# A two-layer model on one core: the shared experts' sums come back into another buffer, and the searched order of the instructions is replaced

## The reference, cut to what matters

```
sh_mid = gelu(einsum('th,ehd->ted', xt, Wsh_up))
shared_out = einsum('ted,edh->th', sh_mid, Wsh_down)
...
routed_out = einsum('ted,edh->th', rt_mid * gate[:, :, None], Wrt_down)
return shared_out + routed_out
```

## Time and profile before

| | us |
|---|---|
| runs: median (lowest to highest) | 1294.34 (1285.93 to 1298.04) |
| the profiled execution's own time | 1290.69 |
| its span, first to last instruction | 1288.9 |
| TensorE busy in the span | 1176.2 (91%) |
| VectorE / GpSimd / ScalarE busy | 1062.3 (82%) / 869.4 (67%) / 841.6 (65%) |
| mean granted TensorE clock | 0.972 of full speed |

### The profile page before, as it was taken

The page is one execution under the profiler, slowest core; times in us unless marked ns, Lnnn a source line. Parts: engine busy times, 40 slices in busy tenths (PEclk is TensorE's granted clock), DMA queues, the critical chain, the costliest instruction groups (busy, mean ns, idle before and its releaser), DMA issues.

```text
span 1288.9 us, 28774 instructions
## 1 busy us (share of the span) xinstructions
PE 1176.2 (91%) x9866; PEld 987.2 (77%) x9866; DVE 1062.3 (82%) x2365; ACT 841.6 (65%) x2393; POOL 869.4 (67%) x1101
## 2 busy tenths in 40 slices
PE   8899889788986999998999899989999999899996
PEld 7665446666875888887888888878788889788885
DVE  5797236968799899888989799888799898789778
ACT  4013643657765678776778767868777878587775
POOL 3123442657778887787887788875888797776636
PEclk9899979989998999999999999999999999999998
DMA  7942102224334637345646364545355563645342
GB/s 232 244 140 67 55 27 95 66 54 106 90 97 106 184 66 217 106 150 141 171 104 193 93 195 112 177 142 166 75 175 147 151 157 109 176 120 155 93 130 69
DMA packets 219493, 165.95 MB, mean 129 GB/s; under 512 B 103572, under 2 KB 186772, under 8 KB 219348
## 3 DMA queue, kind: packets, MB, share of 16 engines
q1 hardware_dynamic: 214612, 149.82, 41.9%
q0 software_dynamic: 4736, 14.29, 3.9%
HBM read 115.71 MB, written 48.16 MB: 127 GB/s over the span
## 4 chain that ended last, share of the span: by engine, by line
PE 39%; DVE 19%; POOL 10%; DMA 10%; issue 8%; ACT 7%; SPq 5%; DVEq 0%; POOLq 0%; another core or an unknown queue 0%; ACTq 0%
PE ps L1359 12%; DMA XYLM<-parked 4%; SPq L1305 4%; DVE yv L2168 3%; DMA WK<-in_WK 3%; PE ps L1757 3%; DVE KQ L2168 2%; PE ps L1421 2%; PE ps L1632 2%; PE ps L1694 1%; PE ps L1724 1%; PE ps L1710 1%; PE ps L1765 1%; PE ps L1467 1%; DVE Mp L2047 1%
## 5 line engine op out<-in xcount | busy, mean ns | idle before, releaser
L2576 ACT ACTIVATE XYLM<-ps 128x512 f16<-128x512 f32 x216 | 125.3, 600 | 54.7 <-PE ps L1667 54.0
L2168 DVE SCALAR_TENSOR_TENSOR yv<-ps,cw,yv 128x511 f32<-128x511 f32 (+2 forms) x192 | 142.8, 745 | 6.5 <-ACT yv L2512 2.7
L2168 DVE SCALAR_TENSOR_TENSOR KQ<-ps,cw,KQ 128x511 f32<-128x511 f32 (+2 forms) x192 | 140.6, 743 | 8.4 <-ACT KQ L2512 6.0
L1359 PE MATMUL ps<-XH,WVh 128*128 128x256 f32 (+1 forms) x384 | 134.6, 351 | 3.3 <-DVE O L2367 1.8
L1359 PE MATMUL ps<-XH,WVl 128*128 128x256 f32 (+1 forms) x384 | 123.6, 322 | 0.0
L1359 PE MATMUL ps<-XL,WVh 128*128 128x256 f32 (+1 forms) x384 | 123.5, 322 | 0.0
L2610 ACT ACTIVATE sq<-O 128x128 bf16<-128x128 f32 x256 | 79.4, 310 | 58.3 <-DVE O L2348 20.1
L2616 ACT ACTIVATE O<-O,small 128x128 f32<-128x128 f32 x256 | 82.6, 408 | 22.4 <-POOL small L2854 21.9
L2298 DVE TENSOR_TENSOR ZL<-ps,cst 128x256 f16<-128x256 f32 x192 | 77.7, 417 | 21.0 <-PE ps L1653 19.5
L2873 POOL TENSOR_TENSOR OGL<-O,OGH 128x512 fp32r<-128x512 f32 x62 | 81.1, 1308 | 5.2
L1359 PEld LDWEIGHTS ps<-XH,WVh 128*128 128x128 f32 x384 | 73.6, 192 | 8.2 <-DVE O L2367 1.9
(11 more groups left out here) (359 smaller groups left out, 4072.6 us busy)
## 6 DMA issues: line engine op xcount, KB each, us to landing
XYLM<-parked SPq DMA_DIRECT2D x56, 512.0 KB
RC<-crow SPq DMA_DIRECT2D x128, 128.0 KB
decayed<-PTE SPq DMA_DIRECT2D x64, 256.0 KB
PT<-decayed SPq DMA_DIRECT2D x64, 256.0 KB
parked<-LM SPq DMA_DIRECT2D x56, 256.0 KB
WV<-in_WV SPq DMA_DIRECT2D x16, 512.0 KB, 4.1
exr<-in_ex SPq DMA_DIRECT2D x16, 384.0 KB, 4.3
WK<-in_WK SPq DMA_DIRECT2D x16, 256.0 KB, 4.7
```

What stands on the lines that cost most here:

```text
L1359: m = pe.matmul(o, a, b, start=c + k == 0, stop=c == 1 and k == 2)
L2168: m = dve.scalar_tensor_tensor(out=dst[:, k:512], in0=ps[:, bk, 0:512 - k], scalar=cw[:, h, j, 3 - k:4 - k], in1=dst[:, k:512], op0=ALU.mu ...
L2576: leave(act.activation(changed(u, k), ps[:, bank("b", u, k), :].rearrange("p (c n t) -> p c n t", c=2, t=1 << (k - 1)), ACT.Copy), "b", u, k)
```

## The change

1. `fld` no longer loads into the memory of `WVh` but into the key and query memory of head 13, `KQ[:, 1]`. It waits for the last product that reads this memory, `KS` of unit 55 (head 13's last chunk), in both batches; before, it waited for all `cv` and `Zt` projections of heads 14 and 15. Its rank in the plan is the same. `WVh` stays where it is.
2. In the plan, the costs of three parts of the block inverse are raised: `iv1` from 3.6 to 3.9, `p8` from 1.15 to 1.55, `q8` from 1.15 to 1.6 us. The instructions are the same.
3. `GRAIN` goes from 0.09700 to 0.0517, and all of `RANK` and `LATER` is replaced. The new numbers are from a search over replays in which the DMAs' landing times are spread at random. So every list, of every engine, can have another order, and the PSUM banks follow. No instruction is added or removed by this.

```
-    GRAIN = 0.09700
+    GRAIN = 0.0517
...
-    P.add(("iv1", h), rank + 0.1, ("DVE", 3.6, (("dg", h), "DMA"), (("xc", h - 1), "ACT") if h > LEAD else None,
+    P.add(("iv1", h), rank + 0.1, ("DVE", 3.9, (("dg", h), "DMA"), (("xc", h - 1), "ACT") if h > LEAD else None,
...
-    P.add(("p8", h), rank + 0.1, ("POOL", 1.15, (("iv1", h), "DVE")))
+    P.add(("p8", h), rank + 0.1, ("POOL", 1.55, (("iv1", h), "DVE")))
...
-    P.add(("q8", h), rank + 0.1, ("POOL", 1.15, (("iv2", h), "DVE")))
+    P.add(("q8", h), rank + 0.1, ("POOL", 1.6, (("iv2", h), "DVE")))
...
-    weights = [(("cv", h, v, b), "PE") for h in (HK - 2, HK - 1) for v in range(2) for b in range(2)]
-    weights += [(("Zt", h, n), "PE") for h in (HK - 2, HK - 1) for n in (0, 2, 4, 6)]
-    P.add(("fld",), 4 * HK - 8, ("SP", 6.0, *weights))
+    P.add(("fld",), 4 * HK - 8, ("SP", 6.0, *[(("KS", 4 * HK - 9, b), "PE") for b in range(2)]))
...
-        total, WVh = twins("total", "WVh", [128, 2, 2, 512])
-        total = total[:].rearrange("p a c n -> p (a c n)").rearrange("p (n d) -> p n d", n=NT)
+        WVh = sb("WVh", [128, 2, 2, 512], F32R)
...
+        total = KQ[:, (HK - 3) % 3].rearrange("p k t -> p (k t)").rearrange("p (n d) -> p n d", n=NT)
...
-                    for k in (HK - 2, HK - 1):
-                        for b in range(2):
-                            w.wait_ge(*full("cv", k, 0, b))
-                            w.wait_ge(*full("cv", k, 1, b))
-                        for n in range(0, NT, 2):
-                            w.wait_ge(*full("Zt", k, n))
+                    for b in range(2):
+                        w.wait_ge(*full("KS", 4 * HK - 9, b))
```

Three entries of the tables, as they were and as they become, show the kind of change:

```
-    "ck3": {"DVE": 1725.51}
+    "ck3": {"DVE": 253.77}
-    "ld": {"DMA": -0.42, "SP": -1480.26}
+    "ld": {"DMA": -180.19, "SP": -410.02}
-    "fup": {"SP": 1.33}
+    "fup": {"POOL": 169.77, "SP": -539.82}
```

More of the change, by code:

```diff
@@ L104 @@
[L104 to L113, removed]
@@ L119 @@
[L119 to L128, removed]
[3 rows of a table removed]
@@ new lines @@
+    "iv1": {"DVE": -424.93}, "iv2": {"DVE": -224.76}, "iv3": {"DVE": -443.76}, "kb": {"POOL": 171.24},
+    "kb:first": {"POOL": 14.23}, "kn": {"ACT": 1374.77, "POOL": 134.84},
+    "kn:first": {"ACT": 275.87, "PE": -156.91, "POOL": -308.37}, "kns": {"ACT": -780.5},
+    "kns:first": {"ACT": -329.63}, "ld": {"DMA": -180.19, "SP": -410.02}, "ld:last": {"DMA": 45.92, "SP": 283.5},
+    "ln1": {"ACT": -20.84, "DVE": 222.58, "PE": -88.46}, "ls": {"DMA": 81.69, "SP": -20.91},
+    "ls:last": {"DMA": 56.89, "SP": 366.03}, "max": {"SP": 2.19}, "mk:0": {"POOL": 433.31}, "mk:1": {"POOL": 219.74},
@@ new lines @@
+    "ov:1": {"DVE": -366.86, "PE": 232.57}, "own": {"DVE": -429.99}, "p1:0": {"DVE": -68.36, "PE": -121.26},
+    "p1:1": {"DVE": 27.26}, "p8": {"POOL": -213.19}, "pd": {"DMA": 325.19, "SP": -895.26},
+    "pd:first": {"DMA": 175.96, "SP": 517}, "pd:last": {"DMA": 313.5, "SP": -493.56},
+    "pf": {"DVE": 172.9, "SP": 243.4}, "pl": {"POOL": 6.37}, "pl:first": {"POOL": 15.59}, "pl:last": {"POOL": -36.33},
+    "pm": {"POOL": 68.09}, "pm:first": {"POOL": 634.35}, "pm:last": {"POOL": 639.07},
+    "pre": {"ACT": -830.11, "DVE": 94.48}, "ps": {"DMA": -177.84, "SP": 3.21},
@@ new lines @@
+    "ps:first": {"DMA": -267.15, "SP": -317.62}, "ps:last": {"DMA": 20.34, "SP": 735.5}, "pt:last": {"DVE": -311.51},
+    "pv:0": {"PE": 8.46}, "pv:1": {"PE": -666.95}, "py": {"POOL": 1261.98}, "py:first": {"POOL": 206.17},
+    "q8": {"POOL": 6.96}, "r": {"DVE": -581.63}, "r:first": {"DVE": -65.75, "PE": -1765.17},
+    "r:last": {"DVE": -57.39, "PE": -1050.4}, "rb:0": {"SP": -298.18}, "rc:0": {"DVE": 1012.4},
+    "rc:1": {"DVE": -121.62}, "rd:0": {"SP": 78.63}, "rd:1": {"SP": 210.21}, "row": {"DMA": -531.58},
@@ new lines @@
+    "row:first": {"DMA": -85.8, "SP": -250.3}, "row:last": {"DMA": 241.31, "SP": -1186.17}, "rt1": {"DVE": 298.72},
+    "sT": {"ACT": -139.9, "PE": 3.29}, "sc:0": {"ACT": -400.63, "PE": 0.38}, "sc:1": {"ACT": 450.62, "PE": -125.1},
+    "sd": {"DVE": 1296.02}, "slot": {"DVE": -98.48, "PE": -539.68}, "so": {"DVE": -153.94, "PE": -273.42},
+    "so:first": {"DVE": 578.75, "PE": -1724.17}, "so:last": {"DVE": 0.93, "PE": -188.84}, "spg": {"POOL": -19.8},
+    "sq": {"ACT": 298.13, "POOL": -483.87}, "sq:first": {"ACT": 126.75}, "sq:last": {"ACT": 593.63},
@@ new lines @@
+    "U:first": {"ACT": 0.06}, "U:last": {"PE": 0.25}, "Vt": {"ACT": 0.38}, "Vt:first": {"ACT": 0.21},
+    "am:0": {"POOL": 0.76}, "am:1": {"POOL": 0.36}, "b:last": {"ACT": 0.25}, "c:last": {"PE": 0.14},
+    "cb": {"DMA": 1.91, "DVE": 0.84}, "ck1:first": {"DVE": 0.07}, "ck3": {"DVE": 0.03}, "ck:first": {"ACT": 0.7},
+    "cnt": {"PE": 0.1}, "cq": {"ACT": 0.04}, "cq:first": {"PE": 0.01}, "crow": {"ACT": 1}, "cv": {"ACT": 0.02},
+    "cv2": {"DVE": 0.27}, "cv2:first": {"DVE": 0.12}, "dd:0": {"SP": 0.2}, "dec": {"POOL": 0.03},
@@ new lines @@
+    "dec:first": {"POOL": 0.12}, "dec:last": {"ACT": 0.04}, "dg": {"DMA": 0.06, "SP": 0.2}, "dn": {"DVE": 0.08},
+    "exg:0": {"ACT": 0.89, "DVE": 0.37}, "exg:1": {"ACT": 0.63, "DVE": 0.71}, "exv:1": {"PE": 0.02},
+    "fWK": {"POOL": 0.23, "SP": 0.15}, "fWO": {"POOL": 0.25}, "fin": {"DVE": 0.26, "SP": 5.15}, "fld": {"SP": 1.61},
+    "fs": {"ACT": 0.58}, "fup": {"SP": 1.55}, "fx": {"POOL": 0.83, "SP": 1.85}, "gg": {"DVE": 0.25},
+    "gram:last": {"DVE": 0.09}, "gt": {"ACT": 0.15}, "kb": {"POOL": 0.3}, "kb:first": {"POOL": 0.9},
@@ new lines @@
+    "kn": {"POOL": 0.12}, "kn:first": {"PE": 0.01, "POOL": 1.14}, "kns": {"ACT": 0.02}, "kns:first": {"ACT": 0.1},
+    "ld": {"DMA": 0.08}, "ld:last": {"DMA": 0.13, "SP": 0.09}, "ln1": {"ACT": 0.04, "DVE": 0.1},
+    "ls:last": {"SP": 1.86}, "nr2": {"DVE": 0.06}, "oc:0": {"ACT": 0.43}, "ol:last": {"POOL": 0.37},
+    "on": {"ACT": 0.2}, "op": {"DVE": 0.05}, "os": {"POOL": 0.02}, "os:last": {"POOL": 0.58},
+    "ot:first": {"PE": 0.01}, "ot:last": {"DVE": 0.47, "PE": 0.4}, "pd": {"DMA": 0.11}, "pd:first": {"SP": 2.09},
@@ new lines @@
+    "pd:last": {"DMA": 0.66, "SP": 2.67}, "pf": {"DVE": 0.64}, "pl:first": {"POOL": 0.05}, "pl:last": {"POOL": 0.75},
+    "ps": {"DMA": 0.34}, "ps:first": {"DMA": 1.8, "SP": 0.14}, "ps:last": {"SP": 1.51}, "py:first": {"POOL": 0.06},
+    "rb:0": {"SP": 2.21}, "rb:1": {"SP": 0.6}, "rc:0": {"DVE": 0.53}, "rd:0": {"SP": 0.58}, "rd:1": {"SP": 2.44},
+    "row": {"SP": 0.47}, "row:first": {"SP": 3.25}, "row:last": {"DMA": 0.31, "SP": 1.09}, "sc:0": {"ACT": 0.44},
+    "sd": {"PE": 0.01}, "slot": {"PE": 0.33}, "small": {"SP": 0.46}, "so:first": {"DVE": 0.02},
@@ L185 @@
+    "so:last": {"DVE": 0.27, "PE": 0.3}, "spg": {"POOL": 1.06}, "sq:first": {"ACT": 0.13},
+    "sq:last": {"ACT": 0.34, "POOL": 0.19}, "sr": {"DMA": 0.44, "POOL": 0.17}, "sw": {"DMA": 0.12},
+    "sx": {"SP": 0.53}, "tp": {"DVE": 1.69}, "up": {"ACT": 0.36}, "x1": {"DVE": 0.1}, "xb": {"SP": 3.52},
+    "xi:first": {"POOL": 0.14}, "y:last": {"DVE": 0.73, "PE": 0.35}, "yl:last": {"DVE": 0.37, "PE": 0.22},
 }
```

95 lines of the change are left out of this document (31 added, 64 removed), and 27 rows, old and new, of tables (LATER, RANK).

## The result

| | before | after |
|---|---|---|
| runs, median (lowest to highest), us | 1293.59 (1285.93 to 1298.04) | 1229.97 (1228.63 to 1230.73) |
| the profiled execution / its span | 1290.69 / 1288.9 | 1230.72 / 1228.9 |
| mean granted TensorE clock | 0.972 | 0.982 |

The account below looks back on a forecast made before the run. TensorE's throughput was taken to bound the middle, the state chain of head 15 and VectorE's and GpSimd's lists the end. 1290.7 - 6 - 4 = 1280.7, on the median's scale 1284; range 1267 to 1306.

Parts of the forecast that it names:

- Part 3: All lists: the new numbers move everything and remove nothing; taken as 0 us, between -43 and +14.
- part 2: Block inverse: raised costs stop TensorE's `a` being placed too early; -4 us, between 0 and -10.4.
- The end of -43: Middle: all 14 windows like the best one, TensorE idle 13.6 us in place of 56.2.
- The waits that were read: TensorE's waits in the middle: landing of inverse matrices 12.7 us in 9, scaled output 12.5 us in 9.
- Part 1: Tail: the load of the shared sums moves up to 69 us earlier; -6 us, between 0 and -10.6.
- the stop of 10.85 us: GpSimd's wait in front of its ninth gather in the tail, which the early load was to remove.
- the seven us between them: Tail: `U` of unit 63 was to follow unit 62's after 5.87 us, not 12.83, so 7.0 us sooner.
- the inverse does not take the gain away as long as VectorE and ScalarE serve it at once: Unit 63's inverse: levels of 1.7 us each, 7.4 us in all, ready at 1262.6 at the earliest.
- the rival of the larger gain: Landing waits to a quarter, scaled-output waits halved, tail gives 10.6 us: 1268 us; chance 0.22 of below 1278.
- Slower: Rival: TensorE's `a` waits for its matrices in every head, 1312 us; chance 0.16 of above 1300.
- The sum fails outright if the busy middle itself gets longer or shorter by more than 10 us: Written test on the middle: a change of more than 10 us either way refutes the forecast sum.
- Extra table loads: ScalarE: silus ahead of the last gates or decays need up to three more loads, 3.8 us, halving the gain at worst.

Follow-up runs that it names:

- a_oldfld: After with the old load of the shared sums, also in the plan, so all lists were made anew with the new numbers: 1243.06 us, ratio 0.9630 to before.
- b_weights: Before without the 28 key/query and output weight loads from head 2 on and without the waits for them; GpSimd's work stays: 1264.73 us, ratio 0.9842.
- b_all: Before without weight loads from head 2 on, with half of each `XYLM` load and `p8`, `q8` on 384 of 512 elements: 1256.98 us, ratio 0.9772.
- b_early: Before's lists, TensorE's untouched, with `fld` in head 13's key memory and gathers, additions, silus and preliminary sums moved forward: 1294.63 us, ratio 1.0039.
- a_late: After's lists, TensorE's untouched, with the old load's memory and wait; gathers, additions, silus and preliminary sums moved behind it: 1245.87 us, ratio 0.9645 to before.
- b_thin: Before's lists with GpSimd's `p8` and `q8` on 384 of 512 elements, so each takes about 1.15 us: 1288.74 us, ratio 0.9975.

## Why the prediction was wrong

- **Part 3, the new numbers: the step that failed.** It took 0, within -43 to +14. Measured: 48 us of 61 with the old load (`a_oldfld`), which holds the new costs of part 2 as well. Choosing the mean of the old windows, "the nearest row", was no argument: the row says what the old order does. The end of -43 was nearly right for the middle, which gave 45.0 us with 86 matmuls fewer in it. The rest was looked for nowhere: the 15 us ahead of head 2, where GpSimd's weight waits were 14.4 us in 3 (1.2 in after) and `b_weights` wins 10.2. Nor did it count that the plan itself could be shorter (20 us), or that busy time shrinks (735.8 to 731.6 to 729.1 for the same matmuls from before to `b_weights` to `b_all`).
- **The waits that were read.** The prediction took the waits of the bounding engine and weighed `XYLM`, 12.7 us. The landings that cost most were those where GpSimd stood, 40.8 and 9.7 us, one view further. Their price shows in the growth of the lag; TensorE's waits for `O` carried only a part of it (12.5 to 6.3 us in the middle of `b_weights`).
- **Part 1: the load came early, what it was to free did not follow.** It was issued at 1126, behind a `KS` of unit 55 that is earlier like all else, additions started at 1136, and of the stop of 10.85 us one of 4.6 is left. But VectorE is busy 33.5 of the last 39 us, where under 30 was expected, `U` of 63 comes 9.2 us after `U` of 62 and not 6, and in `b_early` the seven us between them did not go. Before's own plan has 13.8 us there, so the order itself held the gap. The sentence that failed is "the inverse does not take the gain away as long as VectorE and ScalarE serve it at once": they serve in list order, as TensorE does, and a level took 4.0 to 4.6 us, not 1.7; 4.7 and 5.0 stood in the trace of before. The tail is 0.1 us longer in after. What the early load buys is that head 15's projections may stand in the tail, 11 us by `a_late`, 13 to 15 of the whole by the ratios of `a_oldfld` and `a_late`, an effect the rival of the larger gain named without a price.
- **Part 2: the reason for the -4 fell, the size is open.** `b_thin` gives 0.9975 with an interval that holds 1 and the 4 us, and the waits for `XYLM` stay. It makes the steps as short as planned; the new costs by themselves were not run.
- **The rivals.** That of the larger gain was nearest, with the right sentences (landing waits to a quarter, scaled output halved; both fell further, to 0.2 and 3.4) and an end of 1268, since it counted no more than these waits and the tail's idle time. Slower: its condition, `XYLM` waits above 19 us, turned out 0.2. The test written down, "The sum fails outright if the busy middle itself gets longer or shorter by more than 10 us", is what happened, by 45.
- **Extra table loads** at the silus did not come: one, as before. Their price by the row, 3.8 of 6 us, would have been more than the half that was written.

## What to carry to other kernels

Where an engine works through a list in order, look at the distance between a load and the step that waits for it, on every engine and not only on the one that bounds. A planner that takes one fixed landing time can put the waiting step exactly there (13 of 14 heads with the old numbers, 4 with the new), although its result is wanted long after, and each late landing can then pass to what follows; put such a step some microseconds behind the landing, or let the search see spread landing times. Where a change replaces a whole order, compare the execution with the order's own plan, head by head: the difference that grows points at what the plan did not foresee. And do not take the busiest engine's idle time for all of it: of the 28 us between before's middle and `b_all`'s, with the same work, 6.7 came out of what was counted as TensorE's busy time.

## What the runs showed of the hardware

The same load of 256 KB took from 2.7 to 6.7 us from issue to landing in one execution, and 2.6 to 6.3 in the other; the DMA engines' share in the middle was 0.52 and 0.54. In after's tail the mean granted clock was 0.96 with TensorE busy 35.9 of 42.8 us, in before's 0.86 with 32.2 of 42.8, in `a_late`'s 0.87 with 40.8 of 54.2, in `a_oldfld`'s 0.80 with 39.9 of 56.7; in the middle, with TensorE busy 95 and 98% in before and after, it was 0.99 and 1.00. Such a mean lies between the two levels: 0.80 is four tenths of the stretch at 1.2 GHz and the rest at 2.4. It was lowest where the idle time of the tail was largest (16.8 us in `a_oldfld`, 13.4 in `a_late`, 10.6 in before, 7.0 in after), though `a_late` and before do not differ in it. Idle time that a late load makes may thus be paid a second time, in slower matmuls; the prediction had not counted that, and no run separated it.
